# Attention weights and the 0..127 row moved to a PSUM bank of their own

## What is computed

```python
h = jnp.einsum('nf,fhd->nhd', x, W)              # 8 heads of 32
a_src = jnp.sum(h * att_src, axis=-1)
a_dst = jnp.sum(h * att_dst, axis=-1)
e = jax.nn.leaky_relu(a_src[src] + a_dst[dst], NEG_SLOPE)
e_max = jax.ops.segment_max(e, dst, num_segments=N)
e_exp = jnp.exp(e - e_max[dst])
denom = jax.ops.segment_sum(e_exp, dst, num_segments=N)
alpha = e_exp / (denom[dst] + 1e-16)
out = jax.ops.segment_sum(h[src] * alpha[:, :, None], dst, num_segments=N)
```

## Time and profile before

| | us |
|---|---|
| median of 3 runs | 4719.92 |
| lowest, highest | 4691.74, 4777.75 |
| the profiled execution, its time | 4755.14 |
| its span, first to last instruction | 4753.4 |
| TensorE recorded busy | 3284.8 (69%) |
| VectorE busy | 1894.4 (40%) |
| ScalarE busy | 779.3 (16%) |
| GpSimd busy | 2042.0 (43%) |
| granted clock of TensorE, mean | 0.819 |

### The profile page before, as it was taken

One profiled execution on the slowest core, in us unless ns is written; L12 is line 12 of the kernel. 1 busy time (PEld: TensorE's weight loads), 2 busy tenths in 40 slices (PEclk: granted clock), 3 DMA queues, 4 the chain that ended last, 5 costly groups with the idle time before them and its releaser, 6 DMA issues. The chain is left out here.

```text
span 4753.4 us, 55388 instructions
## 1 busy us (share of the span) xinstructions
PE 3284.8 (69%) x13452; PEld 2406.8 (51%) x13453; DVE 1894.4 (40%) x3658; ACT 779.3 (16%) x1287; POOL 2042.0 (43%) x2020
## 2 busy tenths in 40 slices
PE   1526777677667774439996178888888987465992
PEld 1414444455455553436664166677777773343551
DVE  4225555555444557521112633334444442530113
ACT  0200000000000000103221022222222223211320
POOL 1056665555444540252221266766666640062231
PEclk9757777788777887559998588899999999667996
DMA  2134443333323331143223444444444420024225
GB/s 91 47 113 136 118 129 98 112 114 103 94 85 85 108 90 55 36 149 110 71 71 118 138 127 132 133 132 133 131 130 124 126 84 0 6 85 146 85 83 186
DMA packets 313068, 488.99 MB, mean 103 GB/s; under 512 B 54845, under 2 KB 212862, under 8 KB 312702
## 3 DMA queue, kind: packets, MB, share of 16 engines
q0 software_dynamic: 95232, 263.59, 18.6%
q1 hardware_dynamic: 193344, 183.36, 12.5%
q10 hardware_dynamic: 24352, 40.64, 2.5%
HBM read 404.96 MB, written 82.42 MB: 103 GB/s over the span
## 5 line engine op out<-in xcount | busy, mean ns | idle before, releaser
L770 POOL DMA_INDIRECT room<-h_table,src_idx x784 | 830.6, 1059 | 834.8 <-PE at_pss L948 458.3
L1765 POOL DMA_INDIRECT em_msg<-xn_table,src_idx x784 | 791.9, 1010 | 519.9 <-issue 216.1
L993 PE MATMUL at_ps<-room,at_member 128*128 128x264 f32 x2336 | 737.3, 474 | 84.6 <-DVE at_member L784 39.8
L993 PEld LDWEIGHTS at_ps<-room,at_member 128*128 128x128 f32 x2336 | 524.9, 234 | 235.4 <-DVE at_member L784 51.7
L1846 PE MATMUL em_psa<-em_msg,em_member 128*128 128x256 f32 x2336 | 545.4, 390 | 58.3 <-issue 34.1
L1846 PEld LDWEIGHTS em_psa<-em_msg,em_member 128*128 128x128 f32 x2336 | 455.1, 196 | 133.7 <-issue 44.1
L1839 PE MATMUL em_pse<-em_We,em_attr_t 128*128 128x256 f32 x1552 | 402.0, 413 | 69.2 <-DVE em_msg L1790 38.6
L1839 PEld LDWEIGHTS em_pse<-em_We,em_attr_t 128*128 128x128 f32 x1552 | 314.1, 208 | 135.4 <-issue 49.2
L1892 ACT ACTIVATE em_msg<-em_msg 128x1024 f32<-128x1024 f32 x196 | 207.3, 1058 | 675.4 <-DVE em_msg L1790 484.6
L1790 DVE TENSOR_TENSOR em_msg<-em_pse,em_msg 128x1024 f32<-128x1024 f32 x196 | 234.7, 1220 | 198.0 <-DMA room<-in_x_dram 146.7
L1796 DVE TENSOR_TENSOR acc<-em_psa,acc x146 | 61.7, 423 | 491.9 <-remote 277.1
(11 more groups left out here) (341 smaller groups left out, 3902.7 us busy)
## 6 DMA issues: line engine op xcount, KB each, us to landing
at_dst_row<-dst_flat SPq DMA_DIRECT2D x98, 512.0 KB
em_attr<-in_edge_attr_dram SPq DMA_DIRECT2D x97, 512.0 KB
room<-x_sorted SPq DMA_DIRECT2D x57, 516.0 KB, 3.5
room<-h_table,src_idx POOLq DMA_INDIRECT x784
at_resets<-reset_flat SPq DMA_DIRECT2D x784, 8.0 KB
m0c_rows<-y_table ACTq DMA_DIRECT2D x7, 1792.0 KB, 7.8
em_msg<-xn_table,src_idx POOLq DMA_INDIRECT x784
m1c_rows<-y_table ACTq DMA_DIRECT2D x7, 1792.0 KB, 10.5
```

Of the source, the lines that this page charges most:

```text
L770: pool.indirect_dma_start(msg[:, s, j, :], None, mem.h_table[:, :], bass.IndirectOffsetOnAxis(ap=mem.src_idx[:, c:c + 1].bitcast(u32), axi ...
L993: ins = nc.tensor.matmul(ps_a[:, which, 0:MSG], member[which][:, j, :], msg[:, s, c, :], start=(j == 0), stop=False)
L1765: pool.indirect_dma_start(msg[:, s, j, :], None, mem.xn_table[:, :], bass.IndirectOffsetOnAxis(ap=mem.src_idx[:, c:c + 1].bitcast(u32), ax ...
```

## The change

`ps_r` becomes `ps_w`. Its columns 0 to 127 hold the weights of the step (`weight`, chunks by heads), 128 to 255 a copy of the 0..127 row, put there once by ScalarE (`iota_in`). The weighing takes its second input from `weight` instead of the column beside the messages; the marks read the row from PSUM. ScalarE computes the exponential twice, into `weight` and, as before, into the column, which the products still sum for the denominator; so `weighted` counts two a step. The 8 columns of the scale move to the bank of the crossing. `mark_t` and the later edge stage (L1776) are untouched.

Waits are added that keep two engines out of the new bank at the same time: a first mark waits for the first exponential, the shift for both of the step before, the first products for the second. And `mark_further` now stands before `shift_scores`, which releases the next weights.

```diff
-        ps_r = ctx.enter_context(nc.psum_tensor("at_psr", [P, 512], fp32))
+        ps_w = ctx.enter_context(nc.psum_tensor("at_psw", [P, 512], fp32))
+        iota_in = sem("iota_in")
...
+        scale_of_tile = ps_c[:, 3 * P:3 * P + HEADS]
+        weight = ps_w[:, 0:P].rearrange("p (c h) -> p c h", h=HEADS)
+        iota_row = ps_w[:, P:2 * P]
...
+            dve.wait_ge(iota_in, 1)
...
-                return nc.vector.scalar_tensor_tensor(dst[:, :, :], mem.iota_row[:, :].unsqueeze(1).to_broadcast([P, CB, P]),
+                return nc.vector.scalar_tensor_tensor(dst[:, :, :], iota_row.unsqueeze(1).to_broadcast([P, CB, P]),
...
             def shift_scores(k, s, i):
                 dve.wait_ge(turned_back, k + 1)
+                if not isinstance(k, int) or k > 0:
+                    dve.wait_ge(weighted, 2 * k)
...
                 pairs = body_pairs(dve, mem, b)
+                dve.wait_ge(weighted, 2 * k + 1)
                 dve.wait_ge(first_read, b + 1)
...
             def weigh(k, s, quarter):
-                dve.wait_ge(weighted, k + 1)
                 part = msg[:, s, quarter * HC:(quarter + 1) * HC, :].rearrange("p c (h w) -> p (c h) w", w=HW)
+                by = weight[:, quarter * HC:(quarter + 1) * HC, :].rearrange("p c h -> p (c h)")
                 nc.vector.tensor_tensor(part[:, :, 0:HD], part[:, :, 0:HD],
-                                        part[:, :, HD:HW].to_broadcast([P, HC * HEADS, HD]), ALU.mult).then_inc(msg_done, 1)
+                                        by.unsqueeze(2).to_broadcast([P, HC * HEADS, HD]), ALU.mult).then_inc(msg_done, 1)
...
                 weigh(k, s, 3)
+                mark_further(k, 0, pairs0)
+                mark_further(k, 1, pairs1)
                 if has(1, k):
                     shift_scores(*nxt)
                     scale_less_one(k + 1)
-                mark_further(k, 0, pairs0)
-                mark_further(k, 1, pairs1)
...
-                nc.tensor.matmul(ps_r[:, 0:HEADS], member[0][0:1, 0, :], scale_1[:, :], start=True, stop=True).then_inc(scale_spread, 1)
+                nc.tensor.matmul(scale_of_tile, member[0][0:1, 0, :], scale_1[:, :], start=True, stop=True).then_inc(scale_spread, 1)
...
+                if p == 0 and half == 0:
+                    pe.wait_ge(weighted, 2 * k + 2)
                 pe.wait_ge(msg_done, 4 * k + 2 * p + half + 1)
...
+            nc.scalar.activation(iota_row, mem.iota_row[:, :], ACT.Copy).then_inc(iota_in, 1)
...
                 act.wait_ge(shifted, 2 * k + 2)
+                nc.scalar.activation(weight.rearrange("p c h -> p h c"), shift[:, :, :], ACT.Exp).then_inc(weighted, 1)
                 nc.scalar.activation(weight_col(s), shift[:, :, :], ACT.Exp).then_inc(weighted, 1)
```

More of the change, by code:

```diff
@@ L885, in rescale @@
                 of_tile = tile_at(acc, first).rearrange("p (h w) -> p h w", w=HW)
-                nc.vector.scalar_tensor_tensor(of_tile, ps_r[:, 0:HEADS].unsqueeze(2).to_broadcast([P, HEADS, HW]), 1.0, of_tile,
+                nc.vector.scalar_tensor_tensor(of_tile, scale_of_tile.unsqueeze(2).to_broadcast([P, HEADS, HW]), 1.0, of_tile,
                                                op0=ALU.add, op1=ALU.mult).then_inc(rescaled, 1)
```

## The result

The changed kernel took 4983.1 us (median, 4978.3 to 4989.2) against 4724.3 (4691.7 to 4777.8) of the kernel before beside it: ratio 1.0583, 95% interval 1.0536 to 1.063. It is 259 us slower, where 4723 (4610 to 4850) was forecast. Two later repeats beside the kernel before gave 1.0616 and 1.0611.

A forecast was written before the change was run, and what follows sets the result against it. It took the attention stage to be bound by handovers, with TensorE's results heard late while gathers run. Terms 0 - 41 + 37 + 2 + 5 = +3 us gave 4758, less 35 for run scatter: 4723 us, range 4610 to 4850.

The forecast's parts named there:

- A: Attention stage: weighing and marks, with one SBUF input each, stop holding gathers; taken as 0, bounds -82 and +207 us.
- TensorE loses its relief: Rival, attention stage: unhindered gathers make TensorE's updates late earlier in a batch; +104 us, 4827 us, chance 0.24.
- B: Attention stage: marks of further tiles moved ahead of the shift let their products start earlier; -41 us (27 to 55).
- C: Twelve attention steps with two further tiles: second products start later behind the new order; +37 us, bounds 0 and 37.
- D: Attention stage, small things: second exponential 2 us (0 to 21), PSUM operands 5 (0 to 34), new waits 0.
- The signs named: Expected profile changes, mainly in attention: gather times, waits for L948, late updates and mark waits; the rest unchanged.
- does not do what it says: Rival, attention stage: the marks' scalar read from SBUF still holds gathers; 4682 to 4723 us, chance 0.07.
- remote: Sign: waits for updates long after their maker's recorded end, before L1060 and L858, grow if the slower rival holds.
- the slower rival: Rival, attention stage: TensorE loses its relief when gathers run unhindered; +104 us, 4827 us, chance 0.24.

The follow-up runs named there:

- e1: Changed kernel, but weighing and marks read their second operand from SBUF again, new order kept; with late releases: 4772.4 us, ratio 1.0113.
- e13: Changed kernel plus two GpSimd memsets after the 4th, 8th and 12th gather of a step; with late releases: 4603.5 us, ratio 0.9651.
- e9: Changed kernel plus two GpSimd memsets after the 4th, 8th and 12th gather of a step; without late releases: 4250.4 us, ratio 1.0156.
- f2: Kernel before plus two GpSimd memsets after the 4th, 8th and 12th gather of an attention step; without late releases: 4255.5 us, ratio 1.0168.
- f4: Changed kernel without the attention's gathers from the fifth step on; without late releases: 4213.9 us, ratio 1.0079.
- e14: Changed kernel with both second operands in SBUF and VectorE's old order; with late releases: 4764.1 us, ratio 1.000.
- e10: Changed kernel with both second operands in SBUF and VectorE's old order; without late releases: 4185.4 us, ratio 0.9999.
- e12: Kernel before with a step's gathers in four groups of four, each behind a quarter of the weighing; with late releases: 4675.3 us, ratio 0.9802.
- e5: Kernel before with a step's gathers in four groups of four, each behind a quarter of the weighing; without late releases: 4184.7 us, ratio 1.0004.
- f1: Kernel before with memset pauses in the attention and ahead of the 1st and 5th gather of second-layer message batches; without late releases: 4446.5 us, ratio 1.0633.
- e4: Changed kernel with a step's gathers in four groups of four, each behind a quarter of the weighing; with late releases: 4733.1 us, ratio 1.0043.
- g2: Changed kernel without the attention's gathers from the fifth step on; with late releases: 4476.1 us, ratio 0.9518.

## Why the prediction was wrong

**The step that failed is A.** The prediction had the mechanism and the sign of it in its upper bound: a relief in held gathers, lost in 45 batches at 7.0 - 0.6 - 1.8 us, +207. It took 0 instead. Measured: 219 us between the changed kernel and e1. That 207 comes so near is luck: it was worked out from one pair of waits of ScalarE at L1060, and the loss came at scan_step. The argument for 0 was GpSimd's 458 us of slack. That slack says that nobody waits for the gathers. It does not say that the gathers do nothing to the others, and the bound did not rest on their speed but on what TensorE loses while they run. Two bounds with opposite signs were averaged by a row that spoke about only one of them: slack in GpSimd rules out the gain (-82), not the loss. With A at 207 the forecast would have been 4930, still 53 under the 4983 measured. The rival "TensorE loses its relief" was right, with a chance of 0.24 and half its size (4827); it was to decide from 2 us a step, and 4.6 were lost.

**A's evidence.** Rows 5 and 6 carried it, against the Trainium skill's page "SBUF — State Buffer", section "Who interferes with whom", by which TensorE waits on nobody. By this trace TensorE itself does not wait: it runs on while its semaphores arrive late, and then waits for VectorE (232 us before L985). I had also weighed that a held gather might only be a sign of a lively VectorE. e13 settles that: pauses made by GpSimd alone give more than the holds did. What fails is the step from that sentence to "denser gathers could not hurt TensorE".

**B's wait is gone.** -41 (27 to 55) for the further marks ahead of the shift: L1001's idle time falls by 49.5 us (84.6 to 35.1), and none of it is put down to a mark any more (39.8 before). That is idle time in front of one line; what B alone is worth to the kernel was not measured.

**C's wait is there, at the forecast size.** Twelve steps, +3.07 each: the 36.8 us of L1016 for the copy L1084, twelve waits of 3.1. One of them in the changed kernel's timeline:

```profile
1284.90 1.28 DVE L789 SCALAR_TENSOR_TENSOR at_member<-at_psw,neg_base,dst_e 128x1024 f32<-128x1024 f32 x1 [6.73 <-PE at_ps L1001]
...
1287.83 0.71 PE L1016 MATMUL at_ps<-acc,ident 128*128 x2 [3.07 <-ACT acc L1084]
...
1289.21 3.34 PE L1001 MATMUL at_ps<-room,at_member 128*128 128x264 f32 x7 [0.68 <-ACT acc L1091]
```

The first products end at 1284.76 and the second ones start 4.45 us later; the prediction had 4.5.

**B and C together** were to cancel (-4), and with D the sum was +3. e1, which is the change without A, is 1.13% above the kernel before of its set, +53 us (33 to 73 by its interval). So, with late releases, a second and smaller part of the miss lies here. Without late releases they do, as far as it was tried: e9 and f2, with the same pauses, differ by 5 us, though f4, gathers left out, is 30 us over the kernel before. With late releases e1 is at 1.0113 and e14, which has the old order, at 1.000. That speaks for some 50 us of cost of the order, but the two are from different sets, and in absolute times they are 8 us apart, as forecast. Which of the terms is off stays open.

**D, by what was tried, is right.** The weighing from PSUM takes 1207 ns against 1213, the mark 1279 against 1282: nothing, where 5 was taken and 34 was the bound. e10 and e14 keep the second exponential and the shared crossing bank in the old order: 0.9999 and 1.000.

**The signs named.** The gathers fell to 951 ns, so "does not do what it says" was false. The wait for L948 grew to 758 us; I had said by 80, and it grew by 300, in steps that were longer (4.6 us each). The growth of "remote" I looked for in the wrong place: before L1060 it went from 458.3 to 407.7 us, and before L858 it vanished. It grew where the releases fall into the middle of a batch, at scan_step. Outside the stage nothing changed. That the range ended at 4850 comes from entering the slower rival at half its bound.

## What to carry to other kernels

An engine with slack can still be what costs the others: before making it denser, ask what it does to them while it is busy, and let a bound that no row excludes keep its size. Look in the timeline at when the consumer starts against when the producer is recorded as done, here 9.6 us apart, and in which rhythm that comes back. If it follows the gathers, put short breaks between them and measure, best behind a count that is reached anyway (0.98 in e12, 1.00 in e5). A break where the gathers set the pace costs nearly its full length (f1, 191 of 200 us).

## What was not expected of the hardware

- The same kernel took 4184 us in some sets and 4710 to 4785 in others. In the first no release is late and the kernel before has a granted clock of 0.85 to 0.86 over the span, in the others 0.81 to 0.83. The change costs 5.8% in one condition; in the other, by e9 and f2, which both have pauses, about nothing. What makes a set the one or the other is open. The chip alone need not be it: the runs e1 to e4 and e5 to e10 bear the same chip number, 8, and were of either kind.
- Where it occurs in the attention, lateness needs the gathers (g2: one late scan, 8.8 us after the last of them, then none). It is large where they run unbroken (359 us over 49 scans, 9.6 in the one shown) and nearly gone with 1.12 us of rest after every fourth (13 us; 0.13 from L987's end to L841 in the one shown).
- Why semaphores of TensorE are late then was not found, and nothing here tests a reason.
